# GpSimd waits for the landed rows of group g - 1 before it issues the four gathers of group g

## What is computed

```
def gcn_layer(h, W, b):                        # network 0, used twice
    xt = h @ W
    msg = xt[src] * norm[:, None]              # norm from edge weights and degrees
    return relu(segment_sum(msg, dst, n) + b)

def gcn_conv(h, W, b):                         # network 1, used twice
    m = (h @ W)[src] * norm[:, None]           # norm = dinv[src] * dinv[dst]
    return segment_sum(m, dst, n) + b

x = x + gnn0(layernorm(x));  x = x + ffn0(layernorm(x))     # dense experts
x = x + gnn1(layernorm(x));  x = x + ffn1(layernorm(x))     # routed experts
```

## Time and profile before

| | us |
|---|---|
| runs | 5611.9 and 5638.83, median 5625.36 |
| span of the profiled execution | 5647.3 |
| PE busy | 4017.9 (71%) |
| DVE busy | 3072.1 (54%) |
| POOL busy | 2967.7 (53%) |
| ACT busy | 1485.5 (26%) |
| TensorE clock granted, mean | 0.835 of full |

### The profile page before, as it was taken

One profiled execution on the slowest core, in us unless ns is written; L12 is line 12 of the kernel. 1 busy time (PEld: TensorE's weight loads), 2 busy tenths in 40 slices (PEclk: granted clock), 3 DMA queues, 4 the chain that ended last, 5 costly groups with the idle time before them and its releaser, 6 DMA issues.

```text
span 5647.3 us, 64923 instructions
## 1 busy us (share of the span) xinstructions
PE 4017.9 (71%) x21108; PEld 3177.4 (56%) x21109; DVE 3072.1 (54%) x7978; ACT 1485.5 (26%) x4028; POOL 2967.7 (53%) x3232
## 2 busy tenths in 40 slices
PE   7764555555546676777778977788776778785999
PEld 6653433334335466666666755666655666664766
DVE  7765645555447655555555565555546554443434
ACT  6502322232232222222223322222231111124221
POOL 7736466666656555555640016555556555543233
PEclk9987777776678777777779988899988998997999
DMA  2423433333333222222221013333333332225231
GB/s 89 122 68 93 118 96 97 96 96 96 97 89 87 78 80 79 80 80 80 82 67 34 20 60 87 89 92 90 90 102 97 102 93 84 83 77 176 69 104 54
DMA packets 272106, 489.99 MB, mean 87 GB/s; under 512 B 85684, under 2 KB 176805, under 8 KB 271635
## 3 DMA queue, kind: packets, MB, share of 16 engines
q0 software_dynamic: 139312, 377.94, 23.8%
q1 hardware_dynamic: 125336, 101.03, 5.9%
q10 hardware_dynamic: 7118, 6.83, 0.4%
HBM read 426.41 MB, written 62.17 MB: 87 GB/s over the span
## 4 chain that ended last, share of the span: by engine, by line
PE 39%; another core or an unknown queue 23%; DVE 22%; issue 10%; ACT 3%; DVEq 2%; POOL 1%; DMA 1%; ACTq 0%; SPq 0%; POOLq 0%
PE PSA L1020 11%; PE PSA L1164 5%; DVE ACC L2016 4%; PE PSA L1411 4%; PE PSA L1397 4%; PE PSA L1173 3%; PE PSA L1298 3%; PE PSA L1314 3%; DVE XIN L1989 2%; DVE XT L1989 2%; PE PSA L985 1%; PE PSA L979 1%; DVE WORK L2282 1%; PE PSA L1149 1%
## 5 line engine op out<-in xcount | busy, mean ns | idle before, releaser
L853 POOL DMA_INDIRECT WORK<-tab,SRC x2632 | 2522.8, 958 | 2146.8 <-issue 768.0
L2016 DVE TENSOR_TENSOR ACC<-ACC,PSA 64x256 f32 x1360 | 568.9, 418 | 1457.7 <-remote 959.4
L1020 PE MATMUL PSA<-WORK,XIN 128*128 128x256 f32 x3192 | 960.0, 454 | 458.0 <-ACT XIN L1491 341.5
L1020 PEld LDWEIGHTS PSA<-WORK,XIN 128*128 128x128 f32 x3192 | 711.0, 233 | 612.1 <-issue 492.5
L1020 PE MATMUL PSA<-WORK,XT 128*128 128x256 f32 x2072 | 594.5, 437 | 161.4 <-ACT XT L1491 85.4
L1020 PEld LDWEIGHTS PSA<-WORK,XT 128*128 128x128 f32 x2072 | 439.4, 222 | 248.9 <-issue 172.6
L1149 PE MATMUL PSA<-WORK 128*128 128x256 bf16 x784 | 161.6, 290 | 327.4 <-DVE WORK L2282 98.2
L1173 PE MATMUL PSA<-WORK,XT 128*128 128x42 f32 x832 | 153.8, 350 | 211.8 <-DVE WORK L1989 211.7
L1149 PEld LDWEIGHTS PSA<-WORK 128*128 128x128 bf16 x784 | 69.4, 104 | 379.8 <-issue 230.4
L1989 DVE TENSOR_TENSOR XIN<-PSA,DST 128x512 f32<-128x512 f32 x412 | 279.1, 679 | 2.5 <-DVE PSA L2323 1.4
L1173 PEld LDWEIGHTS PSA<-WORK,XT 128*128 128x128 f32 x832 | 145.8, 260 | 223.7 <-DVE WORK L1989 221.7
(11 more groups left out here) (492 smaller groups left out, 6899.0 us busy)
## 6 DMA issues: line engine op xcount, KB each, us to landing
WORK<-tab,SRC POOLq DMA_INDIRECT x2632
ACC<-in_L_ffn_w SPq DMA_DIRECT2D x16, 1024.0 KB
tab<-WORK SPq DMA_DIRECT2D x98, 128.0 KB
slots_x<-FILL SPq DMA_DIRECT2D x4, 2080.0 KB
ACC<-slots_x SPq DMA_DIRECT2D x8, 910.0 KB
tab<-ACC SPq DMA_DIRECT2D x49, 128.0 KB
WORK<-tab SPq DMA_DIRECT2D x49, 128.0 KB
before_y<-X SPq DMA_DIRECT2D x7, 896.0 KB
```

The source lines that it names most:

```text
L853: po.indirect_dma_start(out=rows[:, 0:width], out_offset=None, in_=tab[:, :], in_offset=bass.IndirectOffsetOnAxis(ap=SRC[:, c:c + 1].bitca ...
L1020: last = pe.matmul(PS[h][:, 0:D], chosen[:, j * P:(j + 1) * P], rows[:, 0:D], start=(j == 0), stop=(j == Q - 1))
L2016: return ve.tensor_tensor(rows, rows, PS[h][half, 0:D], ALU.add)
```

## The change

Before the four gathers of group g, from g = 1 on in each pass, GpSimd waits until all four gathers of group g - 1 have landed. All other waits stay as they were.

```
--- before.py
+++ after.py
@@ -847,6 +847,8 @@
                         po.wait_ge(s_free, 4 + group_of_turn(m - RS_) + 1)
                     if layer == 0 and 2 <= g < ROUND:
                         po.wait_ge(s_dp, RS_ * (g - 1))
+                    if g:
+                        wait_rows(po, layer, g - 1)
                     landed = (s_rx if in_x(layer, g) else s_row)[slot_of(layer, g)]
                     for k, rows in enumerate(rows_of(layer, g)):
                         c = Q * g + k
```

## The result

| | us |
|---|---|
| before, median of 2 runs | 5625.36 (5611.9 to 5638.83) |
| after, median of 2 runs | 6327.66 (6325.36 to 6329.97) |
| ratio | 1.1252, 95% interval 1.1186 to 1.1319 |
| predicted | 5832, range 5690 to 6000 |

The change costs 12.5%. It has the predicted sign, but is over three times the predicted size (702 us for 207), and lies above the range.

A forecast was written before the change was run, and what follows sets the result against it. Bound: the consumer (PE, VectorE), held by unexplained "remote" waits, with GpSimd ahead. Passes +238 and tails -31 gave +207 on the 5647.3 us span, 5854; the profiled span lies 22 above the median, so 5832 us, range 5690 to 6000.

The forecast's parts named there:

- the floor: GpSimd's gathers: after the change a group can't take less than 3 x 1.26 + 2.91 = 6.69, say 6.67 us.
- T: Time from the start of a group's fourth gather until the next group may start; forecast 2.91 us, before at least 1.25.
- The cadence: Time per group between first gathers of successive groups: 6.08 to 6.49 us before, forecast 6.6 to 6.8 in all passes alike.
- the predicted passes: First to last group's first gather, new against old: +112, +36, +43 and +47 us in passes 0 to 3, sum +238.
- The bound worked out: Upper limit of time per group, 3.75 + 3.61 = 7.36 us, from the slowest of three rows; 6.95 was used instead.
- The slots' waits: GpSimd's 930.3 us of waiting for VectorE to give slots back: 857.6 go, 72.7 stay for the degrees.
- The long waits of VectorE: "Remote" waits before VectorE's sums, 959.4 us at line 2016 and 282.2 at 2684; forecast short (under 5 us) and many.
- the pauses don't free the consumer: Rival: PE's results pass only once per group's pause, so pass 1 runs at 8.9 us a group, +355 us, 6187; 10%.
- the tail: Work after the last group's first gather: 12 to 13 us, giving back 16, 8 and 7 in passes 1 to 3.
- The clock: PE's granted clock, 0.73 to 0.90 of full: some loss costs nothing, counted zero, with 100 us left in the range.
- The prediction's estimate from the Trainium skill: DMA from GpSimd, 2.0 us plus bytes over 436 GB/s: 2.3 us for 128 KB, 6.05 us a group, -202 us.
- GpSimd is ahead and not the bound: Kernel before: the ring of slots is full, GpSimd waited 264 times for slots, so PE and VectorE set the time.

The follow-up runs named there:

- first experiment: Changed kernel with its two waits swapped, so the gather itself carries the wait for the rows of g - 1: 5967.33 us, ratio to before 1.0619.

## Why the prediction was wrong

**The step that failed** is the floor: "T is landing plus reaction. Three groups show the same thing with PE as the one that waits". The value of 2.91 us was PE's. PE's reaction after the change is still that, 2.86 and 2.77 us in the rows above, but GpSimd starts 0.70 us later than PE on the same rows. No group inside a pass of the kernel before shows GpSimd's reaction to a wait that stands apart from its gather, and the text gave the wait no cost "beside the time until the rows are there". Measured T is 3.51 us. Of the 0.60 us missed, 0.50 is the place of the wait (first experiment, shown) and 0.10 is the 3.01 us that remain against 2.91. The cadence is also above 3.75 + T = 7.26 by 0.16 us, from groups with a slower gather or landing: 0.10 inside the groups (3.85 on average against 3.75) and 0.06 in T (3.57 against 3.51).

**How much.** Against the predicted passes, the four are over by 188 x 0.72 + 207 x 0.77 + 131 x 0.73 + 131 x 0.79 = 494 us. The predicted span was 5854 and the measured one 6328.3, 474 more. The two agree but for 20 us, of which 18.7 is group 19 of pass 0, which starts at 400.56 and not 419.25; the text had taken that start as fixed.

**The range.** The bound worked out was 7.36 us, from the third landing of the earlier trace rows, and the text used "6.95 as a mean that mixes such groups in". With 7.36 for its end the range would have reached 5832 + 657 x 0.69 = 6285, 43 us short of the result and not 328. The bound was cut by a judgement with no count of such groups behind it. That the measured T of 3.51 lies inside its bounds of 2.76 to 3.61 is luck all the same: the 3.61 came from one slow gather, and the 3.51 from a wait that the sum didn't price.

**What was right.** The slots' waits go (930.3 to 56.2 us). The long waits of VectorE go, and the rival "the pauses don't free the consumer" was false: no cadence of 8.9 us in pass 1, and 7.44 there beside 7.40. They went further than forecast: "remote" waits were to be short and many, and there are none before the sums. The cadence is alike in all passes. The waits stand before 654 groups (some 650 were named), though at 2.63 and not 2.0 us. In pass 1 the tail is 3367.18 + 0.85 - 3355.60 = 12.4 us, in pass 3 11.4, for 12 to 13. The clock was costed at nothing: PE's windows of the earlier trace rows fell from 0.73 and 0.90 to 0.65 and 0.87 in passes 0 and 2 after, and the cadence doesn't follow them:

```profile
400.00:1806.00 1406.00, 810.83 (x2020) 551.17 (x2018) 618.94 (x1849) 347.17 (x1115) 716.49 (x756) 0.65 0.30 80
...
3758.00:4740.00 982.00, 713.89 (x4081) 572.98 (x4082) 469.48 (x1115) 199.71 (x472) 505.34 (x528) 0.87 0.27 79
```

The prediction's estimate from the Trainium skill, "DMA: Bandwidth & Descriptors", section "Anatomy of one DMA — SWDGE (gpsimd) path", would have put T at 2.3 us. No row here is that quick: PE starts 2.77 us after the gather, and GpSimd with the wait as the gather's own 3.01. For T the measurement decides.

**What was right only there.** "GpSimd is ahead and not the bound" is true of a held chip alone. On chip 12, and by its time on chip 0 too, the same program is bound by GpSimd's issue, and the change costs 33% (chip 12). The prediction knew that it didn't know what the "remote" source was; it then took its 959 us as belonging to the kernel, on whatever chip.

## What to carry to other kernels

A wait in front of a row of gathers costs from the last start until the issuing engine itself starts again, and that is to be taken from that engine's rows, with the wait in the form and order that the code will give it: if two waits stand before one instruction, let the one that will really be waited for be the one that the instruction carries (here the one that the code names first). Where a large share of a profile waits for an unknown source, run the unchanged kernel on a second chip before tuning against it: here no version was best on all, since the kernel before is fastest on chips 0 and 12 (4730 us), and the pause before every second group on chip 7 (3.3% under before). A bound that has been worked out belongs in the range whole.

## What the runs showed of the hardware

- **Results of PE held while GpSimd gathers, on some chips.** On chips 2 and 7 before takes 5616 and 5618 us, on chips 0 and 12 4736 and 4727, with the same program and the same 2720 gathers. Where it takes the longer time, sums wait up to 15.7 us for products that are done, ScalarE has such waits too, and pauses end them: 1.3 us of idle time after every four gathers are enough or nearly (one remote wait of 4.9 us is left), 2 us after eight nearly (360.6 us are left of 959.4), 0.85 us after four or 2 us after sixteen are not. The longer the unbroken row, the later the result behind it: 1.45 us behind 4 gathers, 3.71 behind 20. What holds the results, and why only there, no run tells; it may belong to the chips or to a state that they were in at the time.
- **The order of two waits on GpSimd.** 0.5 us for each group whose separate wait is the one really waited for (T 3.51 against 3.01; 0.57 us for each wait between 5520.96 and 5330.0 on chip 0), nothing when it is met (the next group starts 1.25 us after the fourth gather, as before).
- **A held start.** Group 19 of pass 0, which waits for the degrees, starts at 419.25 us before and at 400.56 after. On chips 0 and 12 it starts at 381 to 383 without the change's wait before every group, and at 390.64 with it. That VectorE's degree sums are held there in the same way is likely, but not shown.
